# A four-layer decoder: the FFN self attention with row and column tiles of TensorE, and cross attention masks added by TensorE

## The reference

```
xn = _ln(x, g, b); q, k, v = split(xn @ Wqkv + bqkv)      # 16 heads of 8
scores = einsum('bqhd,bkhd->bhqk', q, k) / sqrt(8)         # 256 x 256 for each batch and head
ctx = einsum('bhqk,bkhd->bqhd', softmax(scores), v)
x = x + ctx @ Wo + bo;  xn2 = _ln(x, ...)                  # then routed experts
```

## Time and profile before

| | us |
|---|---|
| median of three runs | 2258.78 |
| the profiled execution | 2261.14 |
| its span | 2259.4 |
| layer 0 cross attention, scores to close | 566.8 to 623.9 |
| FFN self attention, scores to close | 658.9 to 823.5 |
| layer 1 cross attention, scores to close | 1099.0 to 1141.9 |
| layer 3 cross attention, scores to close | 1750.9 to 1821.0 |

### The profile page before, as it was taken

How to read it: one execution, slowest core, us unless ns; L and a number is a source line. 1 busy time by engine, 2 the same in 40 slices (tenths; PEclk the granted TensorE clock), 3 DMA queues, 4 the chain that set the end, 5 groups by cost and what they waited for, 6 DMA issues and landing times. The chain is left out here.

```text
span 2259.4 us, 25576 instructions
## 1 busy us (share of the span) xinstructions
PE 1642.3 (73%) x9160; PEld 1227.4 (54%) x9160; DVE 1300.3 (58%) x2377; ACT 739.4 (33%) x1362; POOL 385.6 (17%) x411
## 2 busy tenths in 40 slices
PE   3788888896759969994735984966835674876595
PEld 2466666675537656662524973655523662653373
DVE  4699999993755551114566546335245936733853
ACT  1456565651214423321211331012303223333242
POOL 0565655551000000000100000000001005001300
PEclk7799999997869989996767996967967976788597
DMA  5011111101000001000001210000010000000000
GB/s 171 26 34 34 35 34 35 34 13 48 1 0 1 1 0 53 31 10 0 1 0 67 101 56 0 1 1 0 1 75 1 1 1 0 1 1 1 0 1 10
DMA packets 21244, 49.79 MB, mean 22 GB/s; under 512 B 4752, under 2 KB 9232, under 8 KB 20880
## 3 DMA queue, kind: packets, MB, share of 16 engines
q1 hardware_dynamic: 21136, 48.40, 6.4%
HBM read 47.29 MB, written 1.10 MB: 21 GB/s over the span
## 5 line engine op out<-in xcount | busy, mean ns | idle before, releaser
L186 POOL TENSOR_TENSOR rstd<-spread,minus_half 128x4 f32<-128x4 f32 x36 | 36.7, 1020 | 1460.9 <-DVE spread L168 1460.9
L906 PE MATMUL l0h_scores<-l0h_k_rot,l0h_q_slots 128*128 128x128 f32 (+1 forms) x1024 | 206.9, 349 | 0.0
L906 PEld LDWEIGHTS l0h_scores<-l0h_k_rot,l0h_q_slots 128*128 128x128 f32 x1024 | 170.0, 208 | 13.1
L1110 POOL TENSOR_TENSOR l0h_k_part<-large_weights,l0h_sines 128x512 f32<-128x512 f32 x64 | 83.2, 1299 | 219.8 <-PE l0h_scores L906 127.1
L986 ACT ACTIVATE l0h_scores<-l0h_scores,l0h_top 128x128 f32<-128x128 f32 (+1 forms) x256 | 100.4, 392 | 26.1 <-DVE l0h_top L1063 26.0
L1485 DVE TENSOR_TENSOR l0e_weighted<-l0e_out_ps,l0f_weight 128x512 f32<-128x512 f32 x18 | 12.5, 692 | 151.0 <-PE l0e_out_ps L1447 151.0
L882 PE MATMUL l0h_projected<-XT,l0h_wq 128*128 128x256 f32 x256 | 71.0, 401 | 18.9 <-DVE l0h_q_rot L1050 9.8
L1467 ACT ACTIVATE l0e_hidden<-l0e_hidden_ps,l0e_experts 128x512 f32<-128x512 f32 x72 | 49.5, 687 | 107.2 <-PE l0e_hidden_ps L1433 107.2
L1444 PE MATMUL l0e_out_ps<-l0e_experts,l0e_hidden 128*128 128x128 f32 x576 | 82.5, 286 | 0.0
L1057 DVE TENSOR_TENSOR l0h_q_slots<-l0h_q_rot,l0h_chosen 128x1024 f32<-128x1024 f32 x64 | 78.4, 1225 | 7.0 <-DVE l0h_q_rot L1054 0.5
L1111 POOL TENSOR_TENSOR l0h_k_rot<-large_weights,l0h_cosines 128x512 f32<-128x512 f32 x64 | 81.9, 1280 | 0.0
(11 more groups left out here) (682 smaller groups left out, 4057.3 us busy)
## 6 DMA issues: line engine op xcount, KB each, us to landing
l1e_experts<-in_l_experts SPq DMA_DIRECT2D x16, 768.0 KB, 4.2
l0h_chosen<-l0h_chosen_dram SPq DMA_DIRECT2D x64, 128.0 KB, 2.9
l0e_experts<-in_l_experts SPq DMA_DIRECT2D x9, 578.0 KB, 3.8
l0h_pos<-l0h_pos_dram SPq DMA_DIRECT2D x64, 64.0 KB, 2.0
small_weights<-in_w_l_ffn SPq DMA_DIRECT2D x1, 4016.0 KB, 13.4
large_weights<-in_w_l_xattn SPq DMA_DIRECT2D x1, 2632.0 KB, 9.2
l0h_wq<-in_l_wq SPq DMA_DIRECT2D x16, 128.0 KB, 2.9
large_weights<-in_w_l_attn SPq DMA_DIRECT2D x2, 512.0 KB, 6.6
```

Source lines behind the costliest of these rows:

```text
L906: mm = nc.tensor.matmul(at[:, slot], q_slots[:, s % 2, slot, part, i * P:(i + 1) * P], k_rot[:, s % 2, part, 0:KEYS[i][1]], start=False, s ...
L1110: nc.gpsimd.tensor_tensor(k_part[:], source, at_batch(sines, s), ALU.mult)
```

## The change

- FFN self attention: a function of its own, `l0_ffn_attention`, replaces `attention` there. A unit (batch b, p, j) has both query tiles of a batch and two heads (4(p + 2o) + j, o = 0 and 1), whose features lie in two of the four groups of 32 partitions. Still 32 units of 1024 score columns, and 8 blocks to turn.
- Score matmuls contract over 32 rows and stream 256 columns, 4 a unit, in turn from row group p and p + 2, into different PSUM banks. 1/sqrt(8) goes into the keys.
- VectorE only finds the maxima (negated); ScalarE reads the scores in PSUM, with the maximum as bias, 256 columns at a time (4 instructions a unit). There is no subtraction on VectorE.
- The turned blocks are copied half by ScalarE and half by VectorE, into a double buffer.
- In the product the values are the stationary side: 64 columns of a padded value tile (8 of values, 8 of ones, the rest zeros, placed so that four heads add up in one PSUM area), the probabilities stream 256 columns; 4 matmuls a unit, in turn to output partitions 0 to 63 and 64 to 127. So outputs and sums come out transposed, features on partitions.
- After every fourth unit ScalarE copies the sums and VectorE the outputs; after every eighth VectorE takes a reciprocal of 128x256 and multiplies. `close_sublayer` then needs no turning.
- The value tile is filled by GpSimd during the projections, and the values are written in 16 instructions, not 8.
- Cross attentions of layers 0 and 3: the mask tile (0 or -2^100, bf16) is added by one bf16 matmul with an identity per bank (2 a unit, 512 columns each), before the scores accumulate on it. The mask path in `attention` is gone (lines 411 and 413).
- One more constant (bf16 identity); a GpSimd part in `products`, empty elsewhere; shared semaphores in `l3_ffn_rotate`.

```
...
+            nc.gpsimd.memset(k.ident16[:], 0.0).then_inc(filled, 1)
...
-            for m, value in ((k.ident, 1.0), (k.masker, MASKED)):
+            g.wait_ge(filled, 4)
...
-                    if mask:
...
+                    link(v, nc.vector.tensor_reduce(tops, banks, AX.X, ALU.max))
+                    nc.vector.tensor_tensor(packed, banks, bc(tops.unsqueeze(3), full), ALU.subtract)\
                         .then_inc(shifted.sem, 1)
...
             def score(out):
                 for c in range(2):
+                    if mask:
+                        nc.tensor.matmul(out[:, c, :], k.ident16[:], bc(mask(t).unsqueeze(1), [P, HX // 2, SC]),
+                                         start=True, stop=False, skip_group_check=True)
                     mm = nc.tensor.matmul(out[:, c, :], q_t[:, t * P:(t + 1) * P], keys[:, b, c * 8:(c + 1) * 8, :],
-                                          start=True, stop=True)
+                                          start=not mask, stop=True, skip_group_check=True)
...
+            flat = k.sb("l0f_values", [P, T * HX * 64 + 24], F32, att)
+            values = flat[:, 0:T * HX * 64].rearrange("p (t h e) -> p t h e", t=T, h=HX)
+            heads_t = k.sb("l0f_heads_t", [P, N], F32, att)
+
+            by_group = lambda x: x.rearrange("p (o g j) e -> p o g j e", o=2, g=2)
+            own = lambda p: 56 if p else 24
 
             def take_values(v, out):
                 for t in range(T):
+                    for p in range(2):
+                        ins = nc.vector.tensor_tensor(by_group(values[:, t])[:, :, p, :, own(p):own(p) + DX],
+                                                      by_group(out[:, t * P:(t + 1) * P].rearrange(
+                                                          "p (h d) -> p h d", h=HX))[:, :, p],
+                                                      by_group(W("bv").rearrange("p (h d) -> p h d", h=HX))[:, :, p],
+                                                      ALU.add)
                 return ins
+
+            def fill_values(g):
+                nc.gpsimd.memset(values[:, :, :, 0:24], 0.0)
+                nc.gpsimd.memset(values[:, :, :, 32:56], 0.0)
+                for p in range(2):
+                    ones = values[:].rearrange("p t (o g j) e -> p (t o) g j e", o=2, g=2)[:, :, p]
+                    nc.gpsimd.memset(ones[:, :, :, own(1 - p):own(1 - p) + DX], 1.0)
+                nc.gpsimd.memset(flat[:, T * HX * 64:], 0.0)
 
...
+            ], on_gpsimd=fill_values)
...
+                        nc.vector.tensor_scalar(keys[:, j, :], k_t[:], k.own_of_four[:, j:j + 1], DX ** -0.5, ALU.mult,
+                                                ALU.mult)
+
+            l0_ffn_attention(k, q_t, keys, flat, heads_t)
+            close_sublayer(k, "l0f_mid", None, [W("wo")], 1, bias=W("bo"), features_t=[heads_t[:]],
+                           to=(xn[:], xn_t[:]), gain=W("g2"), shift=W("s2"))
...
+def l0_ffn_attention(k, q_t, keys, flat, heads_t):
+    nc = k.nc
+    units = [(b, p, j) for b in range(B) for p in range(2) for j in range(4)]
+    with ExitStack() as ctx:
+        scores = k.ps("l0n_scores", [P, 2, 2, 2, S], ctx)
+        turned = k.ps("l0n_turned", [P, 2, TB, 2, P], ctx)
+        outs = k.ps("l0n_outs", [P, 2, BANK], ctx)
+        probs = k.sb("l0n_probs", [P, 2, 2, 2, S], F32, ctx)
+        probs_t = k.sb("l0n_probs_t", [P, 2, 2, TB * 2 * P], F32, ctx)
...
+        group = lambda o, p: slice(64 * o + 32 * p, 64 * o + 32 * p + 32)
+            @block.tensor
+            def _(pe):
+                def score(u):
+                    b, p, j = units[u]
+                    if u >= 2:
+                        pe.wait_ge(exp_ready.sem, exp_ready.base + 2 * (u - 1))
+                    for i in range(TB):
+                        for o in range(2):
+                            rows = slice(32 * (p + 2 * o), 32 * (p + 2 * o) + 32)
+                            mm = nc.tensor.matmul(scores[:, u % 2, o, i], q_t[rows, (TB * b + i) * P:(TB * b + i + 1) * P],
+                                                  keys[rows, j, b * S:(b + 1) * S], start=True, stop=True)
+                    mm.then_inc(scores_ready.sem, 1)
+                def turn(u, o):
+                    pe.wait_ge(exp_ready.sem, exp_ready.base + 2 * u + o + 1)
+                    if u >= 1:
+                        pe.wait_ge(copied[o].sem, copied[o].base + u)
+                    for c in range(TB):
+                        for i in range(2):
+                            mm = nc.tensor.transpose(turned[:, o, c, i], probs[:, u % 2, o, i, c * P:(c + 1) * P],
+                                                     k.ident[:])
+                    mm.then_inc(turned_ready.sem, 1)
+                def weigh(u):
+                    b, p, j = units[u]
+                    turn_of = u // 4
+                    pe.wait_ge(copied_0.sem, copied_0.base + u + 1)
+                    pe.wait_ge(copied_1.sem, copied_1.base + u + 1)
+                    if j == 0 and turn_of >= 2:
+                        pe.wait_ge(sums_copied.sem, sums_copied.base + turn_of - 1)
+                        pe.wait_ge(rows_copied.sem, rows_copied.base + turn_of - 1)
+                    for c in range(TB):
+                        for o in range(2):
+                            at = ((TB * b + c) * HX + 4 * (p + 2 * o) + j) * 64 + 24 - 8 * j
+                            mm = nc.tensor.matmul(outs[64 * o:64 * o + 64, turn_of % 2, 0:S], flat[:, at:at + 64],
+                                                  probs_t[:, u % 2, o, c * S:(c + 1) * S], start=(j == 0 and c == 0),
+                                                  stop=(j == 3 and c == TB - 1), skip_group_check=True)
+                    mm.then_inc(out_ready.sem, 1)
+                score(0)
+                for u in range(len(units)):
+                    if u + 1 < len(units):
+                        score(u + 1)
+                    if u >= 1:
+                        weigh(u - 1)
+                    turn(u, 0)
+                    turn(u, 1)
+                weigh(len(units) - 1)
+            @block.scalar
+            def _(act):
+                def exponents(u, o):
+                    if o == 0:
+                        act.wait_ge(topped.sem, topped.base + u + 1)
+                        if u >= 2:
+                            act.wait_ge(turned_ready.sem, turned_ready.base + 2 * (u - 1))
+                    for i in range(TB):
+                        last = nc.scalar.activation(probs[:, u % 2, o, i], scores[:, u % 2, o, i], ACT.Exp,
+                                                    bias=top[:, u % 2, o, i:i + 1])
+                    last.then_inc(exp_ready.sem, 1)
+                def copy_turned(u):
+                    act.wait_ge(turned_ready.sem, turned_ready.base + 2 * u + 1)
+                    if u >= 2:
+                        act.wait_ge(out_ready.sem, out_ready.base + u - 1)
+                    nc.scalar.copy(probs_t[:, u % 2, 0], flat_turned(0)).then_inc(copied_0.sem, 1)
+                def copy_sums(turn_of):
+                    b, p = divmod(turn_of, 2)
+                    act.wait_ge(out_ready.sem, out_ready.base + 4 * (turn_of + 1))
+                    for o in range(2):
+                        last = nc.scalar.copy(sums[group(o, p), b % 2], outs[group(o, 1 - p), turn_of % 2, 0:S])
+                    last.then_inc(sums_copied.sem, 1)
+                for u in range(len(units)):
+                    exponents(u, 0)
+                    if u >= 1:
+                        copy_turned(u - 1)
+                    exponents(u, 1)
+                    if u % 4 == 1 and u >= 4:
+                        copy_sums(u // 4 - 1)
+                copy_turned(len(units) - 1)
+                copy_sums(len(units) // 4 - 1)
+            @block.vector
+            def _(v):
+                def find_top(u):
+                    v.wait_ge(scores_ready.sem, scores_ready.base + u + 1)
+                    nc.vector.tensor_reduce(top[:, u % 2], scores[:, u % 2], AX.X, ALU.max, negate=True)\
+                        .then_inc(topped.sem, 1)
+                def copy_turned(u):
+                    v.wait_ge(turned_ready.sem, turned_ready.base + 2 * u + 2)
+                    if u >= 2:
+                        v.wait_ge(out_ready.sem, out_ready.base + u - 1)
+                    nc.vector.tensor_copy(probs_t[:, u % 2, 1], flat_turned(1)).then_inc(copied_1.sem, 1)
+                def copy_rows(turn_of):
+                    b, p = divmod(turn_of, 2)
+                    v.wait_ge(out_ready.sem, out_ready.base + 4 * (turn_of + 1))
+                    for o in range(2):
+                        last = nc.vector.tensor_copy(heads_t[group(o, p), b * S:(b + 1) * S],
+                                                     outs[group(o, p), turn_of % 2, 0:S])
+                    last.then_inc(rows_copied.sem, 1)
+                def finish(b):
+                    v.wait_ge(sums_copied.sem, sums_copied.base + 2 * (b + 1))
```

(42 more changed lines are left out.)

116 lines of the change are left out of this document (47 added, 69 removed).

## The result

The kernel after takes 2178.3 us (median of four, 2177.51 to 2179.63) where the kernel before takes 2259.07 on the same chip: a ratio of 0.9642 (95% interval 0.963 to 0.9655), 80.8 us less. The forecast was 2180.5. The profiled execution takes 2178.43; its span went from 2259.4 to 2176.7, 82.7 less. Page, part 1 (it answers to the earlier trace rows): TensorE lost 60 us of busy time, VectorE 56.

The account below looks back on a forecast made before the run. TensorE's own time was taken to bound the FFN self attention, VectorE layer 3's cross attention. Savings 46 + 2.4 + 10.3 + 20 - 0.4 = 78.3 us gave 2182.8 profiled, 2180.5 as median; range 2168 to 2212.

Parts of the forecast that it names:

- the close: After FFN self attention, up to the statistics: VectorE sets 2.7 us, 16 product instructions of 0.11 lie beside; 2.4 saved.
- Scores 1.06: FFN self attention, each unit: 8 score instructions of 256 columns on two row groups run side by side, 1.06 us.
- Product 1.06: FFN self attention, each unit: 8 product instructions alternating between two output halves run side by side, 1.06 us.
- The rival of serial column tiles: FFN self attention: column tiles do not overlap, product 1.9 us, unit 4.1, whole 2207; chance 0.16.
- Changes of form: FFN self attention: three switches of TensorE's tiling a unit, 0.25 us added (0 to 0.4), in a pitch of 3.25.
- Reciprocal: FFN self attention, VectorE, 128x256: at most 1.9 us, delays the next maximum, costs about 1.5 three times, 4.5 us.
- Hand-overs: FFN self attention: waits hidden with 0.3 to 0.5 us left; rival, they set the pitch, 2203, chance 0.11.
- Start: FFN self attention's first units at the lower clock: first turns at about 4.4 us, until 6.1; unit 1 takes 6.1.
- GpSimd's fill: Value tile filled during the projections: 6 to 18 us against about 8.5, taken to cost nothing.
- Masks: Cross attentions: layer 0 to 46.8 us, 10.3 saved; layer 3 pitch 7.90 to 5.35, 20 saved.
- the rival of masks that gain nothing: Layer 3 cross attention: TensorE becomes the bound at the old pitch, 20 us less saved, 2200; chance 0.03.
- The lower clock for narrow tiles: FFN self attention runs at 1.2 GHz with narrow tiles and turns, about 213 us, whole 2276; chance 0.03.

Follow-up runs that it names:

- the kernel with one half: Against the kernel after: from the second batch on, all eight product instructions of a unit write to one half of the output partitions; 2194.25 us.
- the order kernel: Against the kernel after: a unit's four product instructions for output partitions 0 to 63 first, then the four for 64 to 127, not in turn; 2178.91 us.
- its pieces: Against the kernel after: reciprocals inside the loop cut into four pieces of 64 columns, one a unit, the multiplication in a later unit; 2176.17 us.
- the busy start: Against the kernel after: three matmuls of 512 columns into a spare bank before the first scores, while VectorE spreads the keys; 2174.41 us.
- The kernel with the busy end: Against the kernel after: seven unused matmuls of 256 columns after the last product, beside VectorE's last reciprocal; 2178.79 us.

## Why the prediction was right, and what it mis-sized

- The forecast of the profiled execution was 2182.8, and 2178.4 came. By terms: the attention saved 3.9 more than forecast, layer 3 1.4 more, layer 0 0.65 more, the close 1.7 less. That is 4.25 of the 4.4. As a median the forecast was nearer, 2180.5 against 2178.3, and that is luck: I had taken off the 2.4 us by which the profiled execution lay above its median before, and after the change it lies 0.1 above.
- The bound: TensorE's own time alone counted in the attention, and still does (the windows after; three waits, 3.1 us together, in 80). This held.
- Scores 1.06: 1.06 to 1.07. Product 1.06 where no row showed it: 1.02. The rival of serial column tiles (1.9, 2207) is refuted by the trace, and by the kernel with one half, which shows what it would have been, 1.88 (1.91 was my bound). The Trainium skill (TensorE: Matmul & The Clock Gate, Part 3) was right on the overlap of column groups; the same part says that matmuls start and end strictly in program order. By that, three of four instructions for one tile would have to be through before the first for the other starts; but in the order kernel, one half after the other, the eight take 1.02 us too. Here the measurement decides against the rule, if the eight reach TensorE in the order of the source; how TensorE arranges it no record shows.
- Changes of form: the pitch is 3.10, not 3.25, and 30 x 0.15 = 4.5 us is the largest error of the sum. 0.04 of the 0.15 is the product (1.02); the other 0.11 is the 0.25 for changes of form. Scores and product each hold the change at their end, so only the one behind the turns was left to add, 1.02 - 0.87 = 0.15.
- Reciprocal: 1.75 us (forecast at most 1.9), and it costs 1.11 each (1.5), three times, as its pieces show. Right in place and mechanism. Another 0.18 ahead of each comes from the copy of the outputs, which the prediction had as fitting in.
- Hand-overs: ScalarE's copy ended 0.4 before the product wanted it (684.94 + 0.58 against 685.94), and the cover held. In the unit behind a copy of outputs it was used up: products 1.11 and, ahead of a reciprocal, 1.24 (687.98 to 689.22) after the scores and not 1.06.
- Start: first turns 4.3 us after the first scores and over at 6.2, then 5.8 for unit 1 (forecast 4.4, 6.1, 6.1). Right, and the busy start shows that the clock is the cause: there the first 16 score instructions take 2.00 us and not 3.78.
- The close failed: 2.7 was forecast and 4.41 came. I took 16 product instructions at 0.11, beside VectorE. But TensorE now stands still for 3.45 us ahead of the close, while sums and outputs are copied, inverted and multiplied, where it stood still for 0.77 before; and behind that wait it gets the lower clock (0.61 in the window above). I had the 3.2 us of that tail in my sum, and did not ask what the wait does to the work behind it. The kernel with the busy end shows the cause and the 1.63 us. The first TensorE row of the close before:

```profile
823.48 0.41 PE L458 MATMUL l0f_mid_turned<-ident,l0f_heads_out 128*128 128x128 f32 x2 [0.77 <-PEq L327]
```

- GpSimd's fill took 6.3 us (635.64 to 641.9) against bounds of 6 to 18, and ended before ScalarE's last projection at 643.26; the sixteen value writes took 2.19 us (from 641.47), beside that projection, which runs to 644.37. Both were hidden, as forecast.
- Masks: layer 3 gained all of the 2.70 a unit (2.55 forecast), as VectorE stays the bound and TensorE is busy for 41.2 of 48.7 us, which refutes the rival of masks that gain nothing; layer 0 paid 0.43 a unit on TensorE, as forecast.
- The lower clock for narrow tiles (2276) did not come: 1.00 over 80 us with a third of TensorE's time in turns. The Trainium skill (the same page, Part 4) has it that transposes do not count as activity for the clock; this trace does not decide it, since two thirds of TensorE's time are other matmuls: it shows only that the upper level holds with a third of the time in float32 turns, and that eight of them take 1.02 us at it.

## What to carry to other kernels

Where the contraction or the stationary side uses half of the array or less (32 rows and 64 columns here), pair two such matmuls on different row groups or output halves and put them next to each other; within eight instructions their order did not matter here. Group what has the same form, since each change of form cost 0.15 to 0.2 us. When a change takes work off TensorE around a short idle stretch, look at the granted clock of what follows: matmuls without a use, into a bank that is free, bought 6 of the 9.2 us here (the pieces of the reciprocal the other 3.2). A long VectorE instruction in a tight loop goes into pieces the size of the engine's slack.

## What the runs showed that I had not expected

- The order among tiles does not matter within eight instructions (1.02 and 1.07 us in both orders), but with turns between them the overlap is gone (2 x 1.01).
- The stretch from the experts to layer 1's cross attention, which no edit touches, took 247.5 to 249.9 us, depending on what stood ahead of it. In one kernel this ate a gain of 1.1 us, in another it added 1.0.
- A wait of 1.3 us soon after a restart brought the lower level back for the first product and turns (0.60, 0.54), while stops of about 1 us in the steady loop left it at 1.00.
- VectorE's reciprocal costs 6.8 ns an element at 128x256 (1.75 us), and 0.54 us for 64 columns.
